# Stacks copied head by head under a semaphore each, and the last unit's context turned one step sooner

## The reference

```python
result = (x @ w_qkv).reshape(b, s, 3, 16, 32)        # 16 heads of 32
scores = einsum('bnqd,bnkd->bnqk', q, k) / sqrt(512)
ctx    = einsum('bnqk,bnkd->bnqd', softmax(scores), v)
x = layernorm(x + ctx)
gate, up = fp4_linear(x, w_gate), fp4_linear(x, w_up)   # 512 -> 1408
x = layernorm(x + fp4_linear(silu(gate) * up, w_down))  # 1408 -> 512
```

## Time and profile before

| | us |
|---|---|
| median of 3 runs | 3910.82 |
| lowest and highest run | 3905.0, 3914.27 |
| profiled execution, its own time | 3908.83 |
| its span, from the first to the last instruction | 3907.0 |

### The profile page before, as it was taken

One profiled execution on the slowest core, in us unless ns is written; L12 is line 12 of the kernel. 1 busy time (PEld: TensorE's weight loads), 2 busy tenths in 40 slices (PEclk: granted clock), 3 DMA queues, 4 the chain that ended last, 5 costly groups with the idle time before them and its releaser, 6 DMA issues. The chain is left out here.

```text
span 3907.0 us, 60891 instructions
## 1 busy us (share of the span) xinstructions
PE 3712.1 (95%) x22469; PEld 1716.7 (44%) x22469; DVE 3166.1 (81%) x5203; ACT 1714.1 (44%) x3085; POOL 2201.4 (56%) x1395
## 2 busy tenths in 40 slices
PE   3599999999999999999999999999999999999999
PEld 2244454344544445443544445434454344544354
DVE  9877887788877788778877788877887778877887
ACT  2166423663246632565226642366324663256622
POOL 1289623984259822687228962398424983269822
PEclk9699999999999999999999999999999999999999
DMA  5211101011011110101101110101101111010110
GB/s 169 81 37 34 55 20 39 17 43 49 25 31 32 36 47 20 43 27 40 43 20 39 31 57 20 39 17 42 50 22 33 30 38 47 20 41 27 31 52 22
DMA packets 106561, 152.47 MB, mean 39 GB/s; under 512 B 28176, under 2 KB 55568, under 8 KB 106128
## 3 DMA queue, kind: packets, MB, share of 16 engines
q1 hardware_dynamic: 106256, 148.49, 12.2%
HBM read 76.28 MB, written 19.66 MB: 25 GB/s over the span
## 5 line engine op out<-in xcount | busy, mean ns | idle before, releaser
L606 DVE TENSOR_REDUCE mx<-R 128x1 f32<-128x512 f32 x2080 | 1316.5, 683 | 372.8 <-PE R L700 367.9
L1263 ACT ACTIVATE arena<-SC 128x512 f32<-128x512 f32 x1360 | 756.5, 604 | 348.0 <-PE SC L1548 321.4
L1623 PE MATMUL SC<-wgu,split 128*128 128x512 f16 (+1 forms) x3456 | 714.5, 361 | 0.0
L1146 POOL TENSOR_TENSOR wd<-wd,arena 128x1024 f32<-128x1024 f32 x224 | 535.0, 2414 | 86.5 <-DVE wd L1384 86.5
L1172 POOL TENSOR_TENSOR arena<-arena,sc_h 128x704 f32<-128x704 bf16 (+1 forms) x144 | 177.9, 1250 | 606.2 <-DVE arena L530 606.2
L1623 PEld LDWEIGHTS SC<-wgu,split 128*128 128x128 f16 x3456 | 338.1, 98 | 331.6
L1305 ACT ACTIVATE arena<-SC,gain 128x512 f32<-128x512 f32 (+1 forms) x192 | 125.1, 652 | 809.6 <-PE R L1623 411.4
L1263 ACT ACTIVATE wd<-SC 128x512 f32<-128x512 f32 x688 | 391.2, 604 | 180.6 <-PE SC L1548 168.7
L680 PE MATMUL R<-xT,wqkv 128*128 128x512 bf16 x1632 | 421.7, 381 | 19.5 <-DVE xT L593 13.1
L700 PE MATMUL R<-ks_even,qs_even 96*128 96x512 bf16 x1056 | 396.1, 390 | 41.8 <-DVE mx L606 16.8
L700 PE MATMUL R<-arena 96*128 96x512 bf16 x1024 | 374.0, 382 | 14.6 <-DVE xT L593 8.1
(11 more groups left out here) (139 smaller groups left out, 5501.4 us busy)
## 6 DMA issues: line engine op xcount, KB each, us to landing
x<-n_L_attn_embeddings_dram SPq DMA_DIRECT2D x136, 256.0 KB, 2.8
wd<-wd_kept SPq DMA_DIRECT2D x32, 512.0 KB, 5.2
out_dram<-x SPq DMA_DIRECT2D x64, 256.0 KB, 2.0
ks_even<-split SPq DMA_DIRECT2D x204, 64.0 KB, 2.0
qs_even<-split SPq DMA_DIRECT2D x408, 32.0 KB, 1.8
arena<-split SPq DMA_DIRECT2D x192, 64.0 KB, 2.0
arena<-split SPq DMA_DIRECT2D x384, 32.0 KB, 1.8
wd<-wd_kept SPq DMA_DIRECT2D x16, 384.0 KB, 7.0
```

Of the source, the lines that this page charges most:

```text
L606: nc.vector.reduce_max(mx[:, j:j + 1], ring_of(ring, job)[:, :], AX_X).then_inc(max_done, 1)
L1146: nc.gpsimd.tensor_tensor(acc[u % 2][i], acc[u % 2][i], probs_of(s)[:, hs, :], ALU.add).then_inc(pool_sum, 1)
L1263: nc.scalar.activation(probs_of(s)[:, hd, :], SC[e % SLOTS][:, :], ACT.Exp, scale=SCALE).then_inc(exp_done, 1)
L1623: last = nc.tensor.matmul(GU[kk % 2][which][:, 0:w], xhT[i % 2][:, part_x * KH + k, :], wgu[:, part_w * KH + k, which * I + first:which * ...
```

## The change

Two things are done. In `stack` the loops are swapped, so that the three DMAs of a head follow each other, and each head of each stack has a semaphore of its own; the maxima matmuls wait for a head's stack before the first of its eight (`j` = 0, 8, 16, 24), where the first waited for all four heads. Whoever waited for a whole stack (ACT before it overwrites `split`, DVE before it reuses `split`, SP at the end) now waits for four semaphores where it waited for one. In unit 7 the context of unit 6 is turned at t=3 instead of t=4, and POOL adds it to x after its sums of step 2 instead of step 3.

```diff
--- before.py
+++ after.py
@@ -59,7 +59,6 @@
 Q_STACK, K_STACK = (HI, HI, LO), (HI, LO, HI)
 STACK = len(Q_STACK) * HD
 STACK_M = STACK + 2
-STACK_DMAS = len(Q_STACK) * GROUP
 STACKS = ("k", "q0", "q1")
 MAX_JOBS = 2 * TILES * HALVES
 TILE_K = BANK // P
@@ -94,8 +93,8 @@
         ((3, (2, 3, 4)), (2, 2, 2, 1, 1, 1, 2, 1)), ((3, (5,)), (4, (0,)), (4, 0, 0, 0, 0, 1, 1, 2)),
         ((4, (1, 2, 3)), (0, 2, 2, 2, 2, 2, 2, 0)), ((4, (4,)), (1, 1, 1, 1, 0, 0, 0, 0)))
 SCORES_AT, VALUES_AT = (0, 1, 3, 4), 2
-SUM_STEP, SUM_T_STEP, CTX_STEP = 2, 3, 4
-ADD_TILE, ADD_TILE_LAST = 4, 3
+SUM_STEP, SUM_T_STEP, CTX_STEP, CTX_STEP_LAST = 2, 3, 4, 3
+ADD_TILE, ADD_TILE_LAST = 4, 2
 LN_MOMENTS, LN_SCALE = 5, 6
 X_TURNS = [(UNITS - 3, t) for t in range(1, TILES)] + [(UNITS - 2, 0)]
 
@@ -134,7 +133,7 @@
     other = []
     if u > 0:
         other += [("sumT", u - 1, 0)] if t == SUM_T_STEP else []
-        other += [("ctx", u - 1, 0)] if t == CTX_STEP else []
+        other += [("ctx", u - 1, 0)] if t == (CTX_STEP_LAST if ends else CTX_STEP) else []
     if (u, t) in X_TURNS:
         other += [("xT", X_TURNS.index((u, t)), 0)]
     total = [("sum", u - 1, 0)] if u > 0 and t == SUM_STEP else []
@@ -416,7 +415,7 @@
         qk_hi = sem("qk_hi")
         qk_lo = sem("qk_lo")
         v_done = sem("v_done")
-        stack_loaded = {name: sem(f"stack_loaded_{name}") for name in STACKS}
+        stack_loaded = {(name, hl): sem(f"stack_loaded_{name}_{hl}") for name in STACKS for hl in range(GROUP)}
         max_done = sem("max_done")
         neg_done = sem("neg_done")
         negT_done = sem("negT_done")
@@ -541,12 +540,12 @@
                 which, half = (1, None) if name == "k" else (0, int(name[1]))
                 if ring.qk(g) >= 0:
                     sp.wait_ge(qk_lo, QK_JOBS * ring.qk(g) + STACK_JOBS[name])
-                for row, part in enumerate((Q_STACK, K_STACK)[which]):
-                    rows = slice(row * HD, (row + 1) * HD)
-                    cols = slice(0, S) if half is None else slice(half * BANK, (half + 1) * BANK)
-                    for hl in range(GROUP):
+                cols = slice(0, S) if half is None else slice(half * BANK, (half + 1) * BANK)
+                for hl in range(GROUP):
+                    for row, part in enumerate((Q_STACK, K_STACK)[which]):
+                        rows = slice(row * HD, (row + 1) * HD)
                         dst = ks[g % 2][rows, hl, :] if half is None else qs[g % 2][rows, half, hl, :]
-                        sp.dma_start(dst, split[hl * HD:(hl + 1) * HD, which, part, cols]).then_inc(stack_loaded[name], 16)
+                        sp.dma_start(dst, split[hl * HD:(hl + 1) * HD, which, part, cols]).then_inc(stack_loaded[name, hl], 16)
 
             def stack_maxima(u):
 
@@ -556,9 +555,10 @@
                                  negT[:, part, :]).then_inc(m_loaded, 16)
             return load_x, stack, stack_maxima
 
-        def stacks_done(eng, n_groups, names=STACKS):
+        def stacks_done(eng, n_groups, names=STACKS, heads=range(GROUP)):
             for name in names:
-                eng.wait_ge(stack_loaded[name], 16 * STACK_DMAS * n_groups)
+                for hl in heads:
+                    eng.wait_ge(stack_loaded[name, hl], 16 * len(Q_STACK) * n_groups)
 
         def scalar_ring(act, ring, x_of):
             def x_transposed(t):
@@ -695,8 +695,8 @@
 
                     g, hl = a // 2, j // (UNIT_TILES * HALVES)
                     t, half = divmod(j % (UNIT_TILES * HALVES), HALVES)
-                    if j == 0 and ring.group(g) >= 0:
-                        stacks_done(pe, ring.group(g) + 1, STACKS[2:] if a % 2 else STACKS[0:2])
+                    if j % (UNIT_TILES * HALVES) == 0 and ring.group(g) >= 0:
+                        stacks_done(pe, ring.group(g) + 1, STACKS[2:] if a % 2 else STACKS[0:2], [hl])
                     last = nc.tensor.matmul(ring_of(ring, job)[:, :], qs[g % 2][0:STACK, a % 2, hl, t * P:(t + 1) * P],
                                             ks[g % 2][0:STACK, hl, half * BANK:(half + 1) * BANK],
                                             start=True, stop=True)
```

## The result

| | before, us | after, us |
|---|---|---|
| median of the runs beside each other | 3906.92 (5 runs) | 3886.54 (5 runs) |
| lowest and highest | 3905.0, 3914.27 | 3884.95, 3886.73 |
| profiled execution, its span | 3907.0 | 3884.7 |
| mean granted clock | 0.987 | 0.989 |

The ratio is 0.9944, with a 95% interval of 0.9932 to 0.9956: faster by 0.56%, or 20.4 us. 3885 was forecast.

What follows compares the result with a forecast made beforehand. PE, busy 95% of the span, was taken as the bound, with gains only where it stands or runs at half clock, in unit 7. 3908.8 less 10.1, 6.5 and 7.9 gave 3884.3; 3885 us was predicted, range 3878 to 3898.

Steps and rivals of the forecast that it cites:

- Part one: Start of unit 7: with head 0's copies first, PE's wait for `q0` goes whole; 10.1 us gained.
- Part two: Middle of unit 7: earlier context ends DVE's wait for POOL's addition, shrinking PE's stand at t=6; 6.5 us gained.
- The clock: Unit 7: five falls to half clock go, since PE's stands behind which they begin go or shrink; 7.9 us gained.
- The rival that would have left the falls in place: Falls of the clock stay or come elsewhere; 3892 us, chance 0.16.
- The sum: Profiled execution's 3908.8 us less 10.1, 6.5 and 7.9 is 3884.3; 3885 predicted.
- What would show it: Signs: `q0` wait and DVE's addition wait gone, stand at t=6 0.5 to 0.7 us, unit 7 37 us at clock 1.00.
- no wait for the maxima's copies has grown: Sign: PE's first scores of unit 7 don't wait longer for the two maxima copies; 0.8 us in hand.
- The slower one: Unit 7: POOL stands in front of the addition, waiting for DVE's multiplication, ahead of two sums; 3922 us, chance 0.04.
- the rival by which all is given back later: Gains are lost in the handover to the feed-forward part; 3906 to 3911 us, chance 0.08.

Runs made afterwards that it cites:

- stacks alone: Changed kernel with the context again turned at t=4 and added after the sums of step 3; 3896.89 us, ratio 0.9970 to before.
- old order: Changed kernel with stack copies part by part as before, still a semaphore for each head; 3884.39 us, ratio 0.9938 to before.
- half changes: The kernel before with only the stacks' part, 3896.89 us, or only the context's part of the change, 3896.39 us.
- context alone: Kernel before with only the context turned at t=3 and added after the sums of step 2 in unit 7; 3896.39 us, ratio 0.9968.
- one wait for all heads: Changed kernel, copies head by head, but the first maximum matmul again waits for all four heads; 3893.53 us, ratio 0.9964 to before.
- turn early: Changed kernel with the addition back behind the sums of step 3, the turn still at t=3; 3894.15 us, ratio 0.9970 to before.
- addition early: Changed kernel with the turn back at t=4, the addition still ahead of the sums of step 3; 3926.09 us, ratio 1.0053 to before.
- the last run: Changed kernel with 64 more semaphore instructions on PE at the end of the weights' stage, before the loop; 3886.63 us, ratio 0.9949 to before.

## Why the prediction was right

**Part one, 10.1.** Right within 0.2 us: 305.6 in the stacks alone against 305.4 by the term and the falls counted. But one reason was too strong: that head 0's copies come first was given as what takes the wait away, and the old order does it too.

**Part two, 6.5.** Undersized: 8 x (1.48 - 0.54) = 7.5. The term was read from DVE's wait for the addition; the same paragraph forecast PE's stand to shrink by 0.8 to 0.9 us, and that, not DVE's row, should have been the term. It shrank by 0.94. Where the 0.13 beyond DVE's 0.81 comes from was not followed up.

**The clock, 7.9.** All five falls went, as forecast, and every fall within unit 7 in these traces begins behind one of the stands of the table, none elsewhere in the unit. The two half changes kept two each. The stands in unit 7 of all runs, of 0.5 us or more:

| stand of PE | falls of the clock behind it | in which kernels |
|---|---|---|
| 0.54 at t=6 | 0 of 48 | after, and the five with both halves of part two |
| 0.55 to 1.5 for `q0` | 8 of 21 | before, context alone, one wait for all heads |
| 1.47 to 1.62 at t=6 | 4 of 24 | before, stacks alone, turn early |
| 0.85 or 0.86, some 5 us ahead of the next row's | 0 of 8 | addition early |
| 3.0 at t=6 | 8 of 8 | addition early |

But the link is one of place too. In unit 6 of every batch PE stands for 1.04 us, longer than several of the stands for `q0` behind which the clock fell (0.88 in the context alone, 0.99 and 1.01 in before). PE's timeline in the second batch of before, and the window behind the stand:

```profile
855.78 0.81 PE L680 MATMUL R<-xT,wqkv 128*128 128x512 bf16 x3 [1.04 <-DVE xT L593]
```

```profile
856.00:859.40 3.40, 3.40 (x17) 1.55 (x16) 2.57 (x5) 2.02 (x4) 1.74 (x1) 1.00 0.00 0
```

This stand occurs 80 times in the ten traces, and no fall follows it. So the falls of unit 7 went with its stands, but a stand's length alone doesn't say whether the clock falls, and the prediction's ground, that what is left is shorter than the 0.96 behind which it held, was weaker than it looked: in the kernel before the clock also held behind 1.08 and behind seven of the eight stands of 1.48. The forecast that the falls go is borne out by six kernels without one behind the 0.54; what decides beside the length is not shown.

The Trainium skill, page "TensorE: Matmul & The Clock Gate", section "Why this matters for your kernels", warns only of idle gaps over about 3 us. The row of 3.0 is as it says. The stands of 0.55 to 1.6 us in unit 7 are not: 12 of 53 were followed by a low clock. The 80 of 1.04 us in unit 6 are. The rival that would have left the falls in place (3892) fell with the eight stretches at 1.00.

**The sum.** Unit 7 gave 26.5 where 24.5 was forecast (1.0 of it in part two, 1.0 in small shifts of the unit). Against it stands the term that was missing, 4.3 us given back: 3.0 in the rest of the loop, and 1.3 in the weights' stage. The waits for the maxima's copies grew by 2.4 of it; the rest has no cause shown. Low clock doesn't explain the stage: it had 69.5 us of it where before had 64.2, but the kernels with the old order and with one wait had about 84 and took only 187.5 and 187.7. The sum was 3884.3 and the profiled execution took 3886.54. That this is 2.3 us off and no more is in part luck, for the 2.0 more and the 4.3 less have separate causes.

**What would show it.** All marks came but one: "no wait for the maxima's copies has grown". The argument there was made for unit 7 and held there; the waits grew in the other units, of which the prediction said nothing; in before no such wait is longer than 0.4 us.

**The rivals.** The slower one, made to happen, cost 18.9 us (3926.09 against 3907.15) where the prediction had 13.5 with the stacks' 10.1 gained; the falls of the clock make up more than the difference, nine low stretches where there were five. It did not come about because the product is ready in time: at 899.03, which is 2.11 us behind the turn of the sums at 896.92. Counted from the turn of before, 900.56, that is 902.67, against the 902.6 forecast and the 903.5 at which POOL breaks even. Of the rival by which all is given back later, 4.3 of 26.5 us came true, in the units and not in the handover that it named.

## What to carry to other kernels

Where several engines queue behind one product, move its producer and its consumer together: here, beside the stacks, the early turn alone gave nothing and the early addition alone cost 31 us. A semaphore for each piece that is read first cost PE nothing that could be measured in this kernel, and takes a wait away even if the copies stay in their order. A short stand of PE can be worth more than itself, but it depends on the place: in unit 7, 12 of 53 stands of 0.55 to 1.6 us cost another 1.6 us of half clock, and 80 of 1.04 us in unit 6 cost none. Read the granted clock behind the very stand before you count a gain for it.

## What was not expected of the hardware

- A DMA issue of SP that meets an instruction fetch, by its number PE's (16,384 bytes, about 1.06 us, 181 in a run), can take 0.9 to 1.9 us in place of 0.59; of the stretched issues, 40 of 40 before, 45 of 46 after and 54 of 54 in the last run had one beside them. So did about 60 of the 1272 issues of the usual length, so a packet does not always stretch one. A landing can be late without a stretched issue: one copy of the maxima in the changed kernel landed 3.7 us behind its issue in place of 1.7, and PE stood 1.3 us for it. An edit that adds instructions to PE moves these meetings; PE's waits for the maxima's copies, all at such meetings, were 1.7 us before and 4.1 after.
- The clock's fall behind a short stand doesn't follow from the stand's length: behind 1.47 us before the same matmul, with the same work around, it fell in two batches of eight, and behind 1.04 us in unit 6 in none of 80. What decides it is not shown.
